# Query and key parts of the second layer copied within the chip instead of through memory, and one store of row numbers moved by seventeen tiles

## The reference, cut to what matters

```python
qkv = x @ W_qkv.T
qkv = qkv.reshape(B, T, 3, H, Dh)
scores = jnp.einsum('bhtd,bhsd->bhts', q_c, k_c) * scale
probs = jax.nn.softmax(scores, axis=-1)
```

## Time and profile before

| | |
|---|---|
| Median of three runs | 1700.74 us (1698.26 to 1703.08) |
| The profiled execution | 1698.97 us |
| Its span in the profile | 1696.8 us |
| Mean granted TensorE clock | 0.946 |
| TensorE, VectorE, ACT, POOL busy | 87%, 70%, 49%, 31% |
| DMA moved | 152.84 MB, mean 90 GB/s |

### The profile page before, as it was taken

The page is one execution under the profiler, slowest core; times in us unless marked ns, Lnnn a source line. Parts: engine busy times, 40 slices in busy tenths (PEclk is TensorE's granted clock), DMA queues, the critical chain, the costliest instruction groups (busy, mean ns, idle before and its releaser), DMA issues.

```text
span 1696.8 us, 35053 instructions
## 1 busy us (share of the span) xinstructions
PE 1473.1 (87%) x12952; PEld 934.1 (55%) x12952; DVE 1185.6 (70%) x2666; ACT 823.2 (49%) x1565; POOL 531.9 (31%) x967
## 2 busy tenths in 40 slices
PE   4899998999888798999987988898888898889994
PEld 2566666666666587998873443343444343444431
DVE  4888778788777494455765777777677776778751
ACT  2344344334432333344325656666556665557772
POOL 2422332332331011162314234433434423432223
PEclk7999999999998998999998999999999999999996
DMA  3111111111110656777861345433344433344400
GB/s 109 40 38 45 46 39 45 46 39 45 39 33 26 163 163 200 220 238 215 251 156 51 64 101 101 94 76 71 66 97 101 91 71 73 68 94 83 82 9 12
DMA packets 119082, 152.84 MB, mean 90 GB/s; under 512 B 31348, under 2 KB 83700, under 8 KB 114292
## 3 DMA queue, kind: packets, MB, share of 16 engines
q1 hardware_dynamic: 105992, 120.25, 29.2%
q0 software_dynamic: 12928, 30.43, 6.2%
HBM read 109.01 MB, written 41.09 MB: 88 GB/s over the span
## 4 chain that ended last, share of the span: by engine, by line
PE 55%; DVE 27%; issue 6%; another core or an unknown queue 5%; ACT 2%; SPq 2%; POOL 1%; DMA 1%; DVEq 0%; POOLq 0%; ACTq 0%
PE bank L1766 8%; PE bank L1944 8%; DVE nmax L1471 7%; PE bank L1898 7%; PE bank L1889 7%; PE bank L1967 6%; DVE P L1166 5%; PE bank L1723 3%; PE bank L1666 2%; PE bank L1751 2%; PE bank L1907 2%; PE bank L1783 1%; PE bank L2014 1%; PE bank L1922 1%
## 5 line engine op out<-in xcount | busy, mean ns | idle before, releaser
L1471 DVE TENSOR_REDUCE nmax<-bank 128x1 f32<-128x512 f32 (+3 forms) x704 | 433.9, 636 | 189.0 <-PE bank L1944 144.6
L907 ACT ACTIVATE P<-bank 128x512 f32<-128x512 f32 x640 | 373.8, 597 | 298.8 <-PE bank L1967 230.2
L1944 PE MATMUL bank<-KT,QT 76*128 76x512 bf16 (+3 forms) x1024 | 260.5, 314 | 76.4 <-DVE nmax L1471 48.2
L1967 PE MATMUL bank<-QT,KT 78*128 78x512 bf16 (+3 forms) x1024 | 256.5, 313 | 22.2 <-ACT P L907 13.7
L1944 PEld LDWEIGHTS bank<-KT,QT 76*128 76x128 bf16 x1024 | 88.7, 99 | 265.4 <-DVE nmax L1471 149.2
L609 POOL DMA_INDIRECT xs_d<-xn,idx x128 | 126.1, 985 | 324.0 <-DVE idx L1146 284.6
L1166 DVE TENSOR_TENSOR P<-bank,early_w 128x512 f32<-128x512 f32 x256 | 160.1, 684 | 71.6 <-remote 56.0
L1766 PE MATMUL bank<-P,V 128*32 128x512 f32 (+3 forms) x2048 | 203.4, 471 | 0.0
L871 ACT ACTIVATE hr<-bank 128x512 f32<-128x512 f32 x144 | 86.0, 597 | 192.2 <-PE bank L1889 175.1
L1967 PEld LDWEIGHTS bank<-QT,KT 78*128 78x128 bf16 x1024 | 100.1, 100 | 101.7 <-ACT P L907 39.1
L1435 DVE TENSOR_TENSOR hT<-hr 128x512 f32<-128x512 f32 x144 | 98.2, 691 | 79.1 <-ACT hr L871 77.8
(11 more groups left out here) (233 smaller groups left out, 2263.1 us busy)
## 6 DMA issues: line engine op xcount, KB each, us to landing
P<-in_fc SPq DMA_DIRECT2D x72, 256.0 KB
P<-in_proj SPq DMA_DIRECT2D x72, 256.0 KB
QT<-parts_d SPq DMA_DIRECT2D x96, 192.0 KB
parts_d<-parts SPq DMA_DIRECT2D x32, 384.0 KB, 2.5
P<-xs_d SPq DMA_DIRECT2D x72, 128.0 KB
ys_d<-P POOLq DMA_DIRECT2D x72, 128.0 KB
KT<-parts_d SPq DMA_DIRECT2D x64, 128.0 KB
KT<-parts_d SPq DMA_DIRECT2D x32, 192.0 KB
```

Of the source, the lines that this page charges most:

```text
L907: nc.scalar.activation(P[s % 2][:, u, :], bank[k % 2][:, :], ACT.Exp, scale=float(DH) ** -0.5).then_inc(s_sb, 1)
L1471: nc.vector.tensor_reduce(nmax[:, s // TWO, h:h + TWO * nh - 1:TWO, j], max_bank(n, k)[:, 0:nh * w].rearrange("p (h w) -> p h w", h=nh), A ...
L1944: ins = pe.matmul(max_bank(n, k)[:, i * w:(i + 1) * w], QT[n.p][0:MROWS, h, j * 128:(j + 1) * 128], KT[n.p][0:MROWS, h, 0:w], start=True, ...
L1967: ins = pe.matmul(bank[k % 2][:, c:c + n], KT[b.p][0:SROWS, h, 128 * kb:128 * kb + 128], QT[b.p][0:SROWS, h, 128 * kb:T], start=True, stop ...
```

## The change

It does four things.

1. Within layer 2 (batches 2 to 15), `parts` is no longer stored and loaded back. Instead 18 pieces for each half of the heads are copied from `parts[c]` to `QT` and `KT` inside the chip: one piece is one part for eight rows of the operand, its source 64 rows of 1 KB, its destination 8 rows of 8 KB, 64 KB together. Each waits on SP for a pass of batch b. The pieces of half 0 of batch b+2 go out behind the passes 31 to 39 of batch b, two for a pass, those of half 1 behind the passes 1 to 15 of the following batch, with `shift_rows(b, 1)` between the ninth and the tenth. `load_route` and `load_xa` now stand behind these. Batches 0 and 1 still go through memory.
2. For a half of the heads to be 64 neighbouring rows of `parts`, the rows' order is changed: queries and keys are made with permuted weights, `wqk2`, made by two copies on VectorE at tile 15. The loads of batches 0 and 1 read with a source view that is cut by parts first.
3. ACT's `hi2` of batch 3 and later overwrites `parts`, so it waits for all pieces of the batch before instead of its stores.
4. The store of `idx_all` moves from tile 15 to tile 32, the loads behind it to tile 33.

```diff
@@ constants
+PIECES = [(c, row0 + DH * i, part + i) for c, row0, part, n in LOADS for i in range(n)]
+LATER = 16 * len(PIECES)
...
+        wqk2 = sb("wqk2", [128, 2, 128])
@@ load_half, load_half_at, store_parts2
-                if not n.less(L2 + 2):
-                    sp.wait_ge(s_ps, (n + -2).at(PASS, (h + 1) * PASS // 2 - PASS * L2))
...
-                                 parts_d[n.p, c, part:part + parts_].rearrange("a (d h) t -> (a d) h t", d=DH)[:, hs, :]
+                                 parts_d[n.p, c, part:part + parts_].rearrange("a (f d h) t -> f a d h t", f=2, d=DH)[h]
...
+            def load_half_at(n, h, b, pieces):
+
+                for k, u in pieces:
+                    sp.wait_ge(s_ps, b.at(PASS, u + 1 - PASS * L2))
+                    c, row0, part = PIECES[k]
+                    sp.wait_ge(lo_part, n.at(2, c + 1 - 2 * L2))
+                    sp.wait_ge(s_ps, (n + -2).at(PASS, (h + 1) * PASS // 2 - PASS * L2))
+                    sp.dma_start((QT, KT)[c][n.p][row0:row0 + DH, h * H // 2:(h + 1) * H // 2, :],
+                                 parts[c][64 * h:64 * (h + 1), part, :]).then_inc(half_loaded[n.p][h], 16)
+
             def store_parts2(n):
-                copied = value(sp, n.own(16 * QK_LOADS, -16 * QK_LOADS * HALVES))
...
-                    for h in range(2):
-                        if not n.less(L2 + 2):
-                            sp.wait_ge(half_loaded[n.p][h], copied)
@@ tile
-                if k == STRAIGHT * TB - 1:
-                    sp.wait_ge(rows_ready, 1)
-                    sp.dma_start(idx_d.rearrange("b p k -> p b k"), idx_all[:, :].rearrange("p (b k) -> p b k", b=B)).then_inc(rows_stored, 16)
...
                 if k == LOOPED * TB:
+                    sp.wait_ge(rows_ready, 1)
+                    sp.dma_start(idx_d.rearrange("b p k -> p b k"), idx_all[:, :].rearrange("p (b k) -> p b k", b=B)).then_inc(rows_stored, 16)
+                if k == LOOPED * TB + 1:
                     sp.wait_ge(rows_stored, 16)
@@ body2
+                second_half = within(b + 1) and not b.less(L2 + 1)
+                if second_half:
+                    load_half_at(b + 1, 1, b, [(k, 1 + k * 3 // 4) for k in range(9)])
                 if within(b):
                     shift_rows(b, 1)
+                if second_half:
+                    load_half_at(b + 1, 1, b, [(k, 9 + (k - 9) * 3 // 4) for k in range(9, 18)])
                 if within(b + 4):
                     load_route(b + 4)
                     load_xa(b + 4)
-                if within(b + 2):
-                    store_parts2(b + 2)
                 if within(b + 1):
                     shift_rows(b + 1, 0)
                 if within(b + 2):
-                    load_half(b + 2, 0)
-                    load_half(b + 2, 1)
+                    load_half_at(b + 2, 0, b, [(k, 31 + k // 2) for k in range(18)])
@@ hi2 on ACT
-                if not n.less(L2 + 1):
+                if not n.less(L2 + 3):
+                    for h in range(2):
+                        act.wait_ge(half_loaded[(n + -1).p][h], (n + -1).own(LATER, 16 * QK_LOADS - LATER * HALVES))
+                elif not n.less(L2 + 1):
                     act.wait_ge(parts_stored[c], n.at(16, -16 * L2))
@@ the weights, on VectorE at k == 15
+                    for c in range(2):
+                        nc.vector.tensor_copy(wqk2[:, c, :].rearrange("p (f d h) -> p d f h", f=2, d=DH),
+                                              wqkv2[:, c, :].rearrange("p (d f h) -> p d f h", f=2, d=DH)).then_inc(minus_ready, 1)
@@ q_rows, take_part, max_scores on TensorE
-                pe.matmul(qk_bank(n, c)[:, :], wqkv2[:, c, :], xnT[n.p][:, 1:T + 1], start=True, stop=True).then_inc(qk_ps, 1)
+                if n.less(L2 + 1):
+                    pe.wait_ge(minus_ready, 3)
+                pe.matmul(qk_bank(n, c)[:, :], wqk2[:, c, :], xnT[n.p][:, 1:T + 1], start=True, stop=True).then_inc(qk_ps, 1)
...
-                pe.wait_ge(minus_ready, 1)
...
-                    pe.wait_ge(half_loaded[n.p][half], n.own(16 * QK_LOADS, 16 * QK_LOADS - 16 * QK_LOADS * HALVES))
+                    pe.wait_ge(half_loaded[n.p][half], n.own(LATER, 16 * QK_LOADS - LATER * HALVES))
```

## The result

The changed kernel takes 1726.85 us in the median (1723.23 to 1733.37, four runs), the kernel before 1699.5 (four runs): ratio 1.0168, 95% interval 1.0126 to 1.0209. It is slower by 27 us, where the forecast was 1693, 8 us faster than the median of 1700.74 that it was made against. The profiled span is 1725.7 us against 1696.8, 28.9 more.

The account below looks back on a forecast made before the run. The prediction took TensorE, busy 87% of 1696.8 us, as the bound. From 1698.97 it took 9.7 for tile 15, added 2 for late pieces and 1.8 for the median: 1693 us, range 1672 to 1765.

Parts of the forecast that it names:

- The bubble at tile 15: Expert tiles: moving the idx_all store cuts tile 15's interval from 13.9 to 4.2 us, gaining 9.7 once (bounds 6 to 10.1).
- The moved loads: Tile 33: route and input loads of two batches, issued later, still land 12 us before POOL's need; cost nothing, bound +1.
- The loads of batches 0 and 1: Loads from memory before layer 2, now cut by parts: lateness bounded by 0 and +8 us once, taken as 0.
- My sign for this step: Layer 2's start: the forecast is wrong at the seam if batch 0 starts over 8 us late.
- The price of a piece: Layer 2's copies: each 64 KB piece costs the DMA engines 0.6 us, between 0.49 by bytes and 1.21 by instruction.
- My window: Half 0's eighteen pieces: 12.6 us, from 1232.6 to the first matmul's need at 1245.2, including one landing.
- SP's own price: Issuing pieces in layer 2: 0.44 us each, 7.9 us for 18 copies, so SP barely keeps pace.
- The estimate of 1.2 us for a piece alone: Layer 2's copies: by the skill page's port rule, 64 KB into eight neighbouring partitions at 54 GB/s takes 1.2 us.
- The pause hides a late half: Eleven long batches: 5.7 us of pause, ended by POOL's gathers, makes a late half cost less than its lateness.
- half late: Rival for layer 2's pieces: 0.8 us each, half 0 4.1 us late, +12 to +57, put at 1722 us; chance 0.25.
- ACT's first part of the next queries: ACT's L877 in layer 2: waits for no DMA if the forecast holds, but would wait at 1.21 us a piece.
- Relief: Rival for the long batches: without the load burst half of the 6.9 us gather pause goes, -38, 1655 us; chance 0.10.

Follow-up runs that it names:

- experiment 1: The kernel before with only the store of the row numbers (idx_all) moved from tile 15 to tile 32: ratio 0.9946 (0.9927 to 0.9964).
- experiment 2: The changed kernel with parts_d laid out by half, so batches 0 and 1 load again by 24, 16 or 8 rows outermost: ratio 1.0070.
- experiment 6: The changed kernel without POOL's gathers for batches 3 to 15, whose sums use rows gathered earlier: 1699.37 us, single run.
- experiment 3: The changed kernel with half 0's pieces issued as their own part becomes ready, twelve of them ahead of the shift rows: ratio 1.0166.
- experiment 5: The kernel before without POOL's gathers for batches 3 to 15, whose sums use rows gathered earlier: 1605.71 us beside 1696.86, single run.
- experiment 9: The kernel before with the row numbers' store at tile 32 and POOL's gathers moved behind the layer norm's root: ratio 0.9966 (0.9950 to 0.9981).

## Why the prediction was wrong

**The bubble at tile 15**: right. Forecast 9.7, measured 10.9 at the interval, a little over my bound of 10.1, and 9 us by the ratio of experiment 1. The planning instructions that I left 4.2 us for fitted in 3.0. The moved loads cost nothing, as forecast.

**The loads of batches 0 and 1**: this step failed. I "took 0, with 8 in the range", having looked only at whether they land before they are needed. They did land. What I didn't ask is who stands behind them: the same queue brings every tile's rows. By the changed view a half takes 19.4 us instead of 10.5, the tiles 33 to 71 lost 16.7 us, and undoing the view alone gave 17 back (experiment 2). My sign for this step missed it too: batch 0 starts 7.3 us late, under the 8 that I had set, since the 9.9 us gained ahead of tile 33 stand against it. I had the term of the sum in sight with the view's outer sizes 3, 2 and 1, and put a bound on the wrong waiter.

**The price of a piece**: mis-sized. I took 0.6 us, by bytes, between 0.49 and 1.21. By itself it is 1.08, landing included: 19.5 us for eighteen. The changed kernel's batch 13 has the same, 1554.49 to 1574.41, 19.9 us. My window was right in its end (1569.65 is 5.0 us into the batch, forecast 4.5) and 2 us short at its start: with the store gone from SP's queue the first piece goes out 10.2 us ahead of the batch and not 8.1. So the window is 15.2 us and the half 4.8 late. By my 0.6 it would have been in time. SP's own price was mis-sized as well, 0.72 us a piece (6.48 for nine) where I had 0.44. The row that I had was sixteen loads of different sizes in 19.4 us, and I chose between bytes and instructions by an argument (the pieces' runs are 1 KB "as the loads' are", nothing through memory) whose first half is false. The loads move packets of 8 KB; in the kernel before, 1233 to 1242:

```profile
DMA packets 305, 1.23 MB, mean 136 GB/s; under 512 B 138, under 2 KB 159, under 8 KB 159
```

The estimate of 1.2 us for a piece alone, which the prediction had set against the change, came nearer than my 0.6; but loads into the same eight rows took 0.76 in a row, so no run here shows that the destination's eight rows set the 1.08.

**The pause hides a late half**: right, and shown. The eleven long batches paid nothing (-5.3 us together), the three others 23 us. I had priced the rival "half late" at 0.8 us a piece with three payers at +12; with the real lateness the three pay 10.2, 6.9 and 6.0, the clock's fall behind each wait included, which my sums left out (a wait of 4 us costs 6). Of batch 1's 10.2 some 3 us come only beside gathers, as batch 0's 4.7 do (experiment 6); early pieces remove both (experiment 3), the view put back a part of both (experiment 2), and what the gathers do to them stays open. That ACT's first part of the next queries waits for no DMA was right.

**Relief**: wrong as a rival. The pause is the gathers' own, 91 us of the kernel (experiment 5), and doesn't need the loads (experiment 9).

**The sum** by steps: 1698.97 - 10.9 for tile 15, + 16.7 for the tiles' late rows, + 23.1 for batches 1, 13 and 14, + 4.7 for batch 0, - 5.3 for the long batches, is 1727.3; the remaining 0.1 to the profile's 1727.41 lies in the seam, batch 15 and the early tiles. The outcome lies in the range (1672 to 1765) and near the rival "half late" at 1722, but by other terms: over a third of the loss (16.7 of 44.5 us) came from a step that I had put at zero.

## What to carry to other kernels

For a transfer off the critical path ask two things: does it land in time, and what stands behind it in the queues; here a view whose outermost size is 3 made the first answer "yes" and the second one expensive. A copy's price went by its shape (0.58 to 1.08 us for the same 64 KB), so before many small ones replace few large ones, measure one shape in a row of its own, and read from the trace how long its packets are. And when a change seems free in most repetitions, look for the stall that hides it: if that stall were ever removed, this change would cost 6 us in each of fourteen batches.

## What the runs showed of the hardware beyond that

POOL's eight indirect gathers of a batch, about 10 us of its own time with nobody waiting for their data, make a batch 7 us longer on all other engines, at both places in the batch that were tried (experiments 5 and 9): some 5.7 us of stops on ACT, and some 7 us of TensorE at half its clock behind them. What in a gather does it, POOL's instruction or its transfers, no run took apart. 64 KB within the chip cost 1.08 us for eight rows of destination, in packets of 1 KB, against 0.76 for the same rows from memory in packets of 8 KB. SP also spends more on issuing it: 5.90 us for nine pieces against 3.27 for nine loads of eight rows from memory. And behind a few loads that ran on three engines, three sixteenths of a load of rows (48 of 256 packets) came 7 us after the rest.
